# Second FFN: whole-number weights for gate and up in two passes, group scales by rescaling the sums in PSUM

## The reference, cut to what matters

```python
# x [1024, 512]; gate, up: 512 -> 1376, down: 1376 -> 512; groups of 128 rows of K
w[k, n] = q[k, n] * s[g, n] - (z[g, n] + 1) * s[g, n]      # g = k // 128, q and z whole numbers 0..15
gate, up = x @ Wg, x @ Wu
out = ((gate * sigmoid(gate) * up) @ Wd).astype(float16)
x = layernorm(x + out)
```

## Time and profile before

| | us |
|---|---|
| median of 3 runs (lowest, highest) | 837.18 (836.85, 837.58) |
| profiled execution, in all | 835.33 |
| its span in the profile | 833.6 |
| TensorE busy | 780.0 (94%) |
| VectorE busy | 615.1 (74%) |
| ScalarE busy | 441.4 (53%) |
| GpSimd busy | 308.0 (37%) |
| mean granted TensorE clock | 0.986 |

### The profile page before, as it was taken

The page is one execution under the profiler, slowest core; times in us unless marked ns, Lnnn a source line. Parts: engine busy times, 40 slices in busy tenths (PEclk is TensorE's granted clock), DMA queues, the critical chain, the costliest instruction groups (busy, mean ns, idle before and its releaser), DMA issues.

```text
span 833.6 us, 19024 instructions
## 1 busy us (share of the span) xinstructions
PE 780.0 (94%) x7944; PEld 367.4 (44%) x7944; DVE 615.1 (74%) x875; ACT 441.4 (53%) x597; POOL 308.0 (37%) x235
## 2 busy tenths in 40 slices
PE   8659999887999999999999999999989999999997
PEld 2434444435444444444344444444425544444444
DVE  3999999997565434457769999999966887774344
ACT  4987777636654321143237788778885533332100
POOL 0799999991003000068311223322252122221000
PEclk9699999999999999999999999999999999999999
DMA  6900000005340000059700000000141033310011
GB/s 217 389 5 2 4 3 3 4 4 177 101 120 1 1 1 0 1 79 192 134 2 2 2 2 2 2 2 2 46 141 63 1 123 123 123 61 0 13 38 51
DMA packets 53296, 46.62 MB, mean 56 GB/s; under 512 B 38289, under 2 KB 44241, under 8 KB 53218
## 3 DMA queue, kind: packets, MB, share of 16 engines
q1 hardware_dynamic: 53218, 45.49, 18.8%
HBM read 34.87 MB, written 2.16 MB: 44 GB/s over the span
## 4 chain that ended last, share of the span: by engine, by line
PE 70%; DVE 15%; ACT 6%; issue 4%; POOL 3%; DMA 1%; SPq 1%; DVEq 0%; ACTq 0%; POOLq 0%
PE ps L932 13%; PE ps L696 10%; PE ps L673 9%; DVE arena L1501 8%; PE ps L854 8%; PE ps L968 7%; PE ps L752 6%; PE ps L775 6%; PE ps L831 4%; DVE arena L1717 2%; PE ps L517 2%; PE ps L779 2%; PE ps L583 2%; POOL arena L1329 1%; ACT arena L1228 1%
## 5 line engine op out<-in xcount | busy, mean ns | idle before, releaser
L1717 DVE TENSOR_REDUCE arena<-ps 128x1 f16<-128x512 f32 (+3 forms) x320 | 183.3, 630 | 15.0 <-PE ps L779 6.7
L1228 ACT ACTIVATE arena<-ps 128x1024 f32<-128x1024 f32 (+2 forms) x160 | 143.6, 941 | 36.5 <-PE ps L831 33.6
L1329 POOL TENSOR_TENSOR arena<-arena 128x1024 f32<-128x1024 f32 x62 | 145.4, 2390 | 8.0 <-DVE arena L1501 6.4
L1501 DVE TENSOR_TENSOR_SCAN arena<-arena,ps 128x1024 f32<-128x1024 f32 x64 | 142.1, 2269 | 2.0 <-PE ps L583 0.8
L932 PE MATMUL ps<-arena 128*128 128x512 f16 x528 | 114.6, 379 | 0.1
L696 PE MATMUL ps<-arena 128*128 128x512 f16 (+1 forms) x464 | 97.6, 372 | 1.0 <-ACT arena L1148 1.0
L775 PE MATMUL ps<-arena 64*128 64x512 f16 (+3 forms) x384 | 91.5, 328 | 3.2 <-DVE arena L1717 1.3
L1387 POOL TENSOR_SCALAR_AFFINE_SELECT arena<-arena 128x512 f32<-128x512 f32 x64 | 42.3, 669 | 122.8 <-ACT arena L1228 122.7
L673 PE MATMUL ps<-arena 128*128 128x512 f16 x384 | 87.5, 380 | 0.0
L583 PEld LDWEIGHTS ps<-arena 64*128 64x128 f16 x3072 | 50.6, 97 | 71.7 <-DVE arena L1501 62.5
L1069 ACT ACTIVATE arena<-arena,negA 128x1024 f32<-128x1024 f32 x64 | 72.1, 1144 | 18.8 <-DVE arena L1501 17.8
(11 more groups left out here) (186 smaller groups left out, 967.4 us busy)
## 6 DMA issues: line engine op xcount, KB each, us to landing
arena<-in_w_q_dram SPq DMA_DIRECT2D x11, 768.0 KB, 4.2
arena<-c_rows SPq DMA_DIRECT2D x16, 512.0 KB, 10.7
arena<-in_w_s_dram SPq DMA_DIRECT2D x11, 384.0 KB, 4.9
arena<-in_x_fm_dram SPq DMA_DIRECT2D x8, 256.0 KB, 4.2
out_dram<-arena SPq DMA_DIRECT2D x8, 256.0 KB, 2.0
arena<-in_wg_dram SPq DMA_DIRECT2D x1, 1792.0 KB, 10.0
arena<-in_wu_dram SPq DMA_DIRECT2D x1, 1792.0 KB, 7.4
arena<-in_wd_dram SPq DMA_DIRECT2D x1, 1792.0 KB, 11.3
```

What stands on the lines that cost most here:

```text
L1228: nc.scalar.activation(dst, src, ACT.Exp, scale=float(HD) ** -0.5).then_inc(exp_done, 1)
L1329: nc.gpsimd.tensor_tensor(hC[i % 4][:], hst[i % 3][:], c_all[:, n, :], ALU.mult).then_inc(hc_done, 1)
L1501: nc.vector.tensor_tensor_scan(hst[i % 3][:], dA[i % 3][:], banks(2 * (i % 2), 2), 0.0, ALU.mult, ALU.add).then_inc(scan_done, 1)
L1717: nc.vector.reduce_max(maxima_slot(half, k), ps[:, ring_bank(n), 0:len(heads) * w].rearrange("p (a w) -> p a w", a=len(heads)), AX, negate ...
```

## The change

Gate and up of tiles 1 to 10 no longer carry their scales. Their weight blocks are the whole numbers q - (z + 1), exact in float16, so that two products do (x3h and x3l). The scale enters through the sum: behind the matmuls of group c the sum in PSUM is multiplied, in place, by step_up = s[c] / s[c+1], one number for each output column (a partition here); behind the last group, Silu and the product take s[3] as their scale operand. One output (gate or up of a tile, 1024 tokens, two banks) so takes four passes of four matmuls, and three rescales. Outputs o = 0 to 19 are spread over four slots of two banks, each one pass behind its neighbour (in_turn); in each round of four passes three sums are rescaled or gated. SCALER says who rescales: 50 go to ScalarE, 10 to VectorE. Tile 0 keeps its old three products; its second half fills slots that are empty in the first rounds, and down's products for token tile 0 fill those that are empty in the last.

With that the work of a tile moves about: VectorE makes the whole-number blocks straight from the nibbles (whole_weights, 1024 columns) and the down block's unscaled numbers (512 columns); GpSimd multiplies down's scales (512 columns), writes 256 x the product in float16, casts h and subtracts for h1l (split); ScalarE is left with rescales, Silu, and the casts of the last two tiles. The zero points are taken apart once for all tiles during the first FFN (zero_points), stored to DRAM as bytes and loaded for each tile as one byte a column; unit, its reciprocal and step_up are made there too (units), from scales that a DMA transposes. The loops over m are unrolled. Five buffers of gate and up blocks take the place of two.

```diff
+        def in_turn(r):
+            return [(slot, r - (r - slot) % 4, (r - slot) % 4) for slot in range(4)]
+        PASSES = [(o, c) for r in range(ROUNDS) for slot, o, c in in_turn(r) if 0 <= o < OUTPUTS]
+        SCALER = ("A-AA", "AD-A", "AAA-", "-ADA")
+        SCALED_BY = {(o, c): SCALER[(o + c) % 4][o % 4] for o, c in PASSES if c < DC - 1}
...
             def load_words(m, slot):
-                sp.dma_start(w_zeros[slot][:], w1_z[ds(m, 1), :].broadcast_to([P, NB * P // PACK])).then_inc(ld_w1[slot], 16)
+                sp.dma_start(w_zeros[slot], z_dram[m:m + 1, :].broadcast_to([P, NB * P])).then_inc(ld_w1[slot], 16)
...
+            for m in range(2, M1):
+                sp.wait_ge(w1_nib, m - 1)
+                sp.wait_ge(w1_full, m - 1)
+                sp.wait_ge(w1_scaled, m - 1)
+                load_tile(m, m % 2)
...
+            def gate_up(o, c):
+                m, w = o // 2 + 1, o % 2
+                if c:
+                    pe.wait_ge(scaled[SCALED_BY[o, c - 1]], SCALED_AT[o, c - 1])
+                else:
+                    if o >= 2:
+                        pe.wait_ge((silu1_done, h1_done)[w], m - 1)
+                    if w == 0:
+                        pe.wait_ge(gu_made, m)
+                for part in (x3h, x3l):
+                    for h in range(2):
+                        last = nc.tensor.matmul(banks(2 * (o % 4) + h, 1), gu[(m - 1) % 5][:, w * DC + c, :], part[:, c, h * HALF:(h + 1) * HALF],
+                                                start=(c == 0 and part is x3h), stop=(part is x3l), skip_group_check=True)
+                last.then_inc(pass_done, 1)
...
+            for r in range(ROUNDS):
+                for slot, o, c in in_turn(r):
+                    if o < 0:
+                        w, chunks = next(BESIDE)
+                        first_gate_up(w, 1, chunks)
+                    elif o < OUTPUTS:
+                        gate_up(o, c)
+                    else:
+                        pe.wait_ge(silu1_done, M1 - 1)
+                        down_part(0, next(BEHIND1))
+            down_part(0, (M1 - 2,))
+            pe.wait_ge(silu1_done, M1 - 1)
+            pe.wait_ge(h1_done, M1 - 1)
+            down_part(1, range(M1 - 1))
...
+                    elif SCALED_BY.get((o, c)) == "A":
+                        act.wait_ge(pass_done, PASS_AT[o, c])
+                        col = group_col(o, c)
+                        nc.scalar.activation(banks(2 * slot, 2), banks(2 * slot, 2), ACT.Identity,
+                                             scale=step_up[:, col:col + 1]).then_inc(scaled["A"], 1)
...
+            def down_weights(m):
+                full = w_full[:, 2 * DC * P:]
+                pool.wait_ge(w1_full, m + 1)
+                nc.gpsimd.tensor_tensor(full, full, down_scales[m % 2], ALU.mult).then_inc(w1_scaled, 1)
+                pool.wait_ge(w1_scaled, m + 1)
+                nc.gpsimd.tensor_scalar(wd1[:, 0, m, :], full, WS, None, ALU.mult).then_inc(w1_high, 1)
+
+            def split(m):
+                pool.wait_ge(h1_done, m + 1)
+                nc.gpsimd.tensor_copy(h1h[:, m, :], h132[:, m % 2, :]).then_inc(h1h_done, 1)
+                pool.wait_ge(h1h_done, m + 1)
+                nc.gpsimd.tensor_tensor(h1l[:, m, :], h132[:, m % 2, :], h1h[:, m, :], ALU.subtract).then_inc(h1l_done, 1)
+            down_weights(1)
             keep(2)
+            for m in range(2, M1):
+                down_weights(m)
+                if m >= 4:
+                    split(m - 4)
+            for m in range(M1 - 4, M1 - 2):
+                split(m)
...
             def nibbles(m, u, loads):
                 dve.wait_ge(ld_w1[u], 48 * loads)
-                nib = z_nib[:].rearrange("p (n h) -> p n h", h=2)
-                byte = w_zeros[u][:].bitcast(u8).unsqueeze(2)
-                nc.vector.tensor_scalar(nib[:, :, 0:1], byte, 15, None, ALU.bitwise_and)
-                nc.vector.tensor_scalar(nib[:, :, 1:2], byte, 4, None, ALU.logical_shift_right)
                 nc.vector.tensor_scalar(w_nib[:], w_words[u][:], shift_sb[:, 0:1], 15, ALU.logical_shift_right, ALU.bitwise_and).then_inc(w1_nib, 1)
...
             def unscaled(m):
-                nc.vector.scalar_tensor_tensor(w_full[:], w_nib[:], 1.0, z_nib[:], ALU.subtract, ALU.subtract).then_inc(w1_full, 1)
+                cols = slice(2 * DC * P if m else 0, 3 * DC * P)
+                nc.vector.tensor_tensor(w_full[:, cols], w_nib[:, cols], w_zeros[m % 2][:, cols], ALU.subtract).then_inc(w1_full, 1)
...
+            def whole_weights(m):
+                if m > 5:
+                    dve.wait_ge(pass_done, PASS_AT[2 * (m - 6) + 1, DC - 1])
+                nc.vector.tensor_tensor(gu[(m - 1) % 5].rearrange("p b n -> p (b n)"), w_nib[:, 0:2 * DC * P], w_zeros[m % 2][:, 0:2 * DC * P],
+                                        ALU.subtract).then_inc(gu_made, 1)
...
+            def down_low(m):
+                dve.wait_ge(w1_high, m + 2)
                 nc.vector.scalar_tensor_tensor(wd1[:, 1, m, :], w_full[:, 2 * DC * P:], WS, wd1[:, 0, m, :],
                                                ALU.mult, ALU.subtract).then_inc(w1_low, 1)
...
+            for r in range(ROUNDS):
+                for slot, o, c in in_turn(r):
+                    if o % 2 and c == DC - 1 and o < OUTPUTS and r > 0:
+                        product1(o // 2 + 1)
+                    elif SCALED_BY.get((o, c)) == "D":
+                        dve.wait_ge(pass_done, PASS_AT[o, c])
+                        col = group_col(o, c)
+                        nc.vector.tensor_scalar(banks(2 * slot, 2), banks(2 * slot, 2), step_up[:, col:col + 1], None,
+                                                ALU.mult).then_inc(scaled["D"], 1)
+                    if slot == 1 and r % 2 == 0 and r // 2 + 3 < M1:
+                        nibbles(r // 2 + 3, (r // 2 + 3) % 2, (r // 2 + 3) // 2 + 1)
+                        whole_weights(r // 2 + 3)
+                    if slot == 1 and r % 2 and (r + 3) // 2 < M1:
+                        down_low((r + 3) // 2)
+                        if (r + 5) // 2 < M1:
+                            unscaled((r + 5) // 2)
```

More of the change, by code:

```diff
@@ L921, in second_turn, with first_gate_up @@
                 last.then_inc(x_turned, 1)
[L923 to L936, removed]
+            def first_gate_up(w, h, chunks=tuple(range(DC))):
+                for c in chunks:
+                    for s, part in ((0, x3h), (0, x3l), (1, x3h)):
+                        last = nc.tensor.matmul(banks((4, 6)[w] + h, 1), gu0[:, s, w * DC + c, :], part[:, c, h * HALF:(h + 1) * HALF],
+                                                start=(c == 0 and s == 0 and part is x3h), stop=(c == DC - 1 and s == 1))
+                if h == 1 and chunks[-1] == DC - 1:
+                    last.then_inc((gate1_done, up1_done)[w], 1)
@@ new lines, in down_part @@
+            def down_part(t, ms):
+                for m in ms:
+                    if m < M1 - 2:
+                        pe.wait_ge(h1l_done, m + 1)
+                    else:
+                        pe.wait_ge(h1l_last, m - (M1 - 3))
+                    for part, s in ((h1h, 0), (h1l, 0), (h1h, 1)):
+                        last = nc.tensor.matmul(banks(t, 1), part[:, m, t * P:(t + 1) * P], wd1[:, s, m, :],
+                                                start=(m == 0 and part is h1h and s == 0), stop=(m == M1 - 1 and s == 1))
+                return last
@@ L945, in _ @@
             pe.wait_ge(xl_done, 2 * TT + TT // 2)
-            gate_up1(0, 0, (0,), first=True, only=(0,))
+            first_gate_up(0, 0)
             second_turn(5)
@@ L1866, in _, with low @@
+            def low(m):
+                dve.wait_ge(h1h_last, m - (M1 - 3))
+                nc.vector.tensor_tensor(h1l[:, m, :], h132[:, m % 2, :], h1h[:, m, :], ALU.subtract).then_inc(h1l_last, 1)
+            down_low(1)
             nibbles(2, 0, 2)
+            whole_weights(2)
             unscaled(2)
-            ffn1(0, 0, True)
-            weights_low(2, 0)
-            nibbles(3, 1, 2)
-            unscaled(3)
-            ffn1(1, 1, True)
-            with dve.Fori(1, M1 // 2 - 1) as k:
-                for u in range(2):
-                    weights_low(2 * k + u + 1, 1 - u)
-                    nibbles(2 * k + u + 2, u, k + 2)
-                    unscaled(2 * k + u + 2)
-                    ffn1(2 * k + u, u, False)
@@ L1886, in _ @@
+            low(M1 - 1)
             norm_stage(3, 1.0 / WS, turn=False)
```

177 lines of the change are left out of this document (99 added, 78 removed).

## The result

The changed kernel takes **814.37 us** (median of 4 runs, 813.06 to 815.58) beside 837.01 us (836.40 to 837.58) for the kernel before in the same runs: ratio 0.973, 95% interval 0.9715 to 0.9746. The forecast was 812.8 us in a range of 805.5 to 820. The profiled execution took 813.95 us, with a span of 812.2.

What follows compares the result with a forecast made beforehand. The prediction took TensorE's unbroken matmuls from 662.20 us on as the bound. It summed -34.6 (matmuls removed), +10.9 (port waits), +0.3 and -1.0 (other edges) to -24.4 us: 812.8 us, range 805.5 to 820.

Steps and rivals of the forecast that it cites:

- What is removed: TensorE, gate and up of tiles 1 to 10: 160 fewer matmuls at 0.2162 us each, 34.6 us saved.
- The clock's case: Rival: waits in the second FFN let TensorE's clock fall to 1.2 GHz, giving 876 us; chance 4%.
- What is added on ScalarE and VectorE: Second FFN's gate and up: ScalarE 3.0 of 3.46 us a round, VectorE some 5.75 of 6.92 us a tile.
- the product by 256: GpSimd's multiply of down's weights into float16: unseen form, between 0.6 and 1.16 us, taken as a 0.62 us copy.
- The port: GpSimd and VectorE's SBUF operations exclude each other in gate and up: four rounds take 16.9 us, not 13.84; +10.9 us.
- a load: Tile loads go out about 8 us before nibbles wants them; a late one would stop VectorE; nothing was charged.
- The bank read: Start of down: its third token tile needs the first tile's bank read; +0.3 us, bounds 0 and 0.9.
- Attention's end: Zero-point operations gone and subtract split, easing the lock on GpSimd's selects: -1.0 us, bounds 0 and -1.5.
- The port hardly costs: Rival: waits in gate and up fall where VectorE would have idled, giving 802 to 806 us; chance 12%.
- ScalarE as the bound: ScalarE's in-place rescale at 1.6 us would set the second FFN's pace, giving 821 us; within a 15% rival.
- A slower form: Rival: GpSimd's casts at twice the copy (819 us) or ScalarE's rescale at 1.6 us (821 us); chance 15%.
- Table loads: Rival: Identity and Silu in different sets, each gate adding two 1.28 us loads, some 816 us; chance 3%.

Runs made afterwards that it cites:

- run 1: Changed kernel with GpSimd's four operations per tile of the second FFN replaced by memsets of the same outputs (output not the reference's): 803.31 us, ratio 0.9602.
- Run 3: Changed kernel with down's weights kept without the factor 256, so GpSimd's multiply becomes a casting copy: 813.60 us, ratio 0.9714.
- run 9: Changed kernel with GpSimd's subtract of 1024 columns cut into two of 512 columns: 813.40 us, ratio 0.9724.
- run 4: Changed kernel with all rescales on ScalarE and a casting copy in place of GpSimd's multiply by 256: 807.93 us, ratio 0.9652.

## Why the prediction was right

**What is removed: right.** From the first high and low products (655.56 after, 655.11 before) to the end of down's row (806.83 after, 828.23 before) the stretch shrank from 173.12 to 151.27 us, by 21.9. The forecast's terms with the measured waits, -34.6 + 12.5, give -22.1. The granted clock is 1.00 in the stage, and the matmuls run 0.2162 apart wherever they run (56 of them take 12.26 us in the chain: 55 steps and the 0.38 of the last). The clock's case did not come about, at a busy share of 90% (97.18 of 108.00).

**What is added on ScalarE and VectorE: right.** 1.09 for the rescale (taken 1.10), 1.00 from start to start in a row (taken 1.0); 1.29 and 1.28 for VectorE's rescale and product (taken 1.27); 1.22, 0.69 and 0.68 for whole_weights, unscaled and down_low when alone.

**GpSimd: one term mis-sized.** The cast (1.04 alone) and the subtract (2.13) are as forecast, the scale product 1.15. But the product by 256 takes **1.49 us alone, not 0.62**, above even the upper bound of 1.16. GpSimd's sum for a tile is 5.8 us, not 4.96.

**The port: right in what it does and in its sum, by errors that cancel.** Four rounds take 16.83 us, forecast 16.9. But VectorE's own work is 12.0 in them and not 11.5 (I had taken off too much for overlap), its waits 4.8 and not 5.3, and these lie elsewhere: 2.6 at down_low (1.86 and 0.74), which was given 0.3; nothing at unscaled, given 1.9; 1.2 at nibbles, given 0.45; 1.0 at whole_weights, given 2.65. TensorE's waits in four rounds were 1.9 for one rescale and 1.1 for a product, forecast 2.0 and 0.8 for two rescales and 0.25 for a product. The step that failed is the listing of which instruction waits behind which; that the sum came out at 16.9 all the same is luck. What run 1 shows is the cause and the size of the loss, not this listing. Run 3, which has the 0.61 us that I had assumed, shows the 1.8 on the first whole_weights, and still takes 17.27, more than with the slower form; and it denies the forecast's remark that the waits are most sensitive to GpSimd's unseen forms, at least for this one. Over the stage TensorE's waits on this account came to 11.9 us, forecast 10.9. Within the missing 1.0 lies a load, where I took nothing:

```profile
673.61 1.19 DVE L1865 TENSOR_SCALAR arena<-arena,shift_sb 128x1536 int32<-128x1536 int32 x1 [1.56 <-DMA arena<-in_w_s_dram]
```

The forecast had the loads go out 8 us before nibbles wants them. This one, tile 3's, is issued at 668.26, since SP waits for GpSimd's scale product, which waited for the port and ended at 668.17 (1.98 us for 1.15); VectorE wants it at 672.05. TensorE's next wait, 1.1 us in front of 677.25, ends with the product behind these nibbles, so up to 1.1 us of the 11.9 may be the load's. That is read from the trace and was not tried. One more slip: without the 0.15 us taken off each time, the forecast's 7.4 us for a tile would be 8 x 0.15 = 1.2 us more, not 0.3.

**The other edges.** The bank read costs 0.3, as forecast; the 0.25 for the last remainder of h was not in the forecast. Attention's end: GpSimd's selects are off the chain there, and from the last group of scores (L865 at 622.84 after, L831 at 621.30 before) to the transpose of 626.71 and 626.26 it is 1.1 us shorter, forecast 1.0. No run undid this part alone.

**Where the rest of the miss went.** -34.6 + 12.5 - 1.1 = -23.2, forecast -24.4; the medians lie 22.6 apart, so 0.6 stays unplaced. The profiled executions lie only 21.4 apart. In that of after, TensorE's granted clock is 0.83 over 400 to 410 us, behind a gap of some 1.2 us in which it waits for a DMA. Six matmuls of the first FFN there take 2.74 us instead of 1.47, so this is the 1.2 GHz level for a while. The kernel before has the same gap and 1.00 behind it. TensorE's instructions in that stretch are the same in both, in the same order, and the 1.3 us or so are lost before the stage is reached. A second such stretch of after, 196 to 200 us (0.57, where before has 1.00), goes with another 0.6: there its lead over the kernel before falls from 0.95 (190.50 against 191.45) to 0.33 us (204.32 against 204.65). The profiles of all ten experiments show the lower level somewhere between 404 and 411 us as well; of the kernel before there is one profile, and that execution was also 1.7 us under its median, so it may be the exception. Why the clock falls in one execution and not in another stays open.

**The rivals.** "The port hardly costs" (802 to 806) is what run 1 gives without GpSimd's reads, 803.3: right as a price, wrong as a case. ScalarE as the bound: excluded by its 21.7 us of waiting. A slower form: GpSimd's product by 256 did take 2.4 times the copy, and the loss was not 17 but 11.9; run 3 shows that its price hardly counts. Table loads: two in the stage (1.28 each), one in front of tile 0's Silu (668.28) and one behind the last cast; no later gate adds one.

## What to carry to other kernels

Where two engines share a port and both work in order, add the waits to the row of the engine on which the bound engine depends, and compare the sum with the bound's period; once that row is full, a cheaper instruction, a changed order or a shorter turn moves the waits from one instruction to another and gains little (0.8 to 1.0, 0 to 1.6 and 0.7 to 1.0 us in the medians here, each within its intervals, and mostly in the first rounds). What helps is to take work off that row, or to take away whole turns of the other engine: with the rescales on ScalarE 5.4 us were gained, and 8.6 where GpSimd only wrote h's two parts. Price an unseen form of GpSimd from the same operation with the same types, not from a copy.

## What the runs showed of the hardware that was not expected

- GpSimd's multiplication of 512 columns by a constant, float32 to float16, takes 1.49 us when alone; the casting copy of the same columns 0.61; the two-input product of 512 columns 1.15 (into float32), and run 9's two-input subtract into float16 1.16. Multiplying by a constant is dearer here than either. The Trainium skill ("GPSIMD Engine Reference", section "Engine selection") has operations with one input at roughly line rate; the section gives no time for one. The casting copy goes from 0.61 at 512 to 1.04 us at 1024 columns, 0.84 ns a column, while the product by a constant takes 2.4 times as long as the copy of as many columns. Both have one input, so the trace agrees at most for the copy.
- Who starts first by the profile does not always get the port (GpSimd's times in it are rough): nibbles starting at 704.66 took 2.01 us, against 1.01 alone, beside a scale product of GpSimd that started at 704.71 and took its clean 1.16 (run 3). In run 4 the nibbles at 696.60 took 1.01 and GpSimd's copy at 696.67 1.41 for 0.61: there the first to start had the port, at a distance of 0.07 us against 0.05.
- Where both engines had a port instruction ready, they took turns, one instruction each: run 9's halves with down_low and unscaled between and behind them. Cutting an instruction gave the other engine an earlier turn and a second wait.
